# The expert inputs' transposes go from DMA to TensorE for pairs 18 to 111

## The reference

```python
xn = _layernorm(x)                                   # [8, 512, 256]
# s: attention over columns: softmax(q^T k / sqrt(8)), 256 x 256 per batch
q, k, v = xn @ Wq, xn @ Wk, xn @ Wv
s = swap(softmax(swap(q) @ k / sqrt(8)) @ swap(v)) @ Wo
# f: 32 experts, each row goes to 6 of them (chosen within its 3 best groups of 4)
scores = softmax(xn @ gate_weight.T)
combine = top 6 of the scores in the top 3 of 8 groups, divided by their sum
y = sum over e of combine[:, e] * ((silu(xn @ w1[e].T) * (xn @ w3[e].T)) @ w2[e].T)
shared = silu(xn @ sw1.T) * (xn @ sw3.T) @ sw2.T
out = x + s * silu(y + shared)
```

## Time and profile before

| | us |
|---|---|
| median of 3 runs | 707.58 (707.14 to 709.71) |
| the profiled execution | 710.04 |
| its span, first to last instruction | 708.3 |
| PE busy | 536.7 (76%) |
| DVE busy | 436.6 (62%) |
| POOL busy | 379.8 (54%) |
| ACT busy | 303.8 (43%) |

### The profile page before, as it was taken

One profiled execution on the slowest core, in us unless ns is written; L12 is line 12 of the kernel. 1 busy time (PEld: TensorE's weight loads), 2 busy tenths in 40 slices (PEclk: granted clock), 3 DMA queues, 4 the chain that ended last, 5 costly groups with the idle time before them and its releaser, 6 DMA issues.

```text
span 708.3 us, 12537 instructions
## 1 busy us (share of the span) xinstructions
PE 536.7 (76%) x3308; PEld 386.9 (55%) x3308; DVE 436.6 (62%) x1380; ACT 303.8 (43%) x626; POOL 379.8 (54%) x401
## 2 busy tenths in 40 slices
PE   7687885959586787842999888887887877888860
PEld 6465664647374666521877565554554545655540
DVE  7976786959595958860332355565564556555566
ACT  5434654554545453521454334334333344343341
POOL 1175665666656666763002655565555656655654
PEclk9868998989899798955999989999999999999995
DMA  9999392938484343533999999999999999999975
GB/s 328 413 393 397 154 390 94 355 149 303 188 287 173 119 171 112 174 123 104 219 236 217 224 284 271 256 297 288 269 268 274 289 247 266 303 288 274 268 231 168
DMA packets 216514, 174.69 MB, mean 247 GB/s; under 512 B 128770, under 2 KB 201218, under 8 KB 215554
## 3 DMA queue, kind: packets, MB, share of 16 engines
q1 hardware_dynamic: 192514, 108.30, 59.7%
q0 software_dynamic: 18432, 50.36, 21.4%
q10 hardware_dynamic: 5504, 15.24, 5.8%
HBM read 52.20 MB, written 92.27 MB: 204 GB/s over the span
## 4 chain that ended last, share of the span: by engine, by line
PE 41%; another core or an unknown queue 18%; ACT 15%; issue 12%; DVE 10%; DMA 2%; POOL 2%; ACTq 0%; POOLq 0%; DVEq 0%; SPq 0%
PE ps L760 11%; PE ps L780 8%; PE ps L675 7%; PE ps L659 6%; PE ps L667 3%; ACT early L616 3%; PE ps L681 3%; PE ps L770 2%; ACT work L594 2%; ACT work L609 2%; DVE work L1062 1%; POOL early L454 1%; DVE acc L1043 1%; ACT L535 1%
## 5 line engine op out<-in xcount | busy, mean ns | idle before, releaser
L454 POOL DMA_INDIRECT early<-slots_d,slot_at x192 | 186.6, 972 | 184.3 <-DMA slots_d<-early 58.0
L760 PE MATMUL ps<-w_all,work 128*128 x1344 | 190.0, 281 | 41.3 <-issue 27.1
L760 PEld LDWEIGHTS ps<-w_all,work 128*128 128x128 f16 x1344 | 115.6, 100 | 106.3 <-issue 80.8
L1062 DVE SCALAR_TENSOR_TENSOR work<-ps,work 128x256 f32<-128x256 f32 x112 | 47.2, 421 | 180.3 <-ACT work L594 172.2
L436 POOL DMA_INDIRECT slots_d<-early,slot_at x96 | 96.0, 1000 | 80.2 <-DVE slot_at L914 29.4
L436 POOL DMA_INDIRECT slots_d<-work,slot_at x96 | 95.0, 990 | 55.2 <-issue 25.4
L594 ACT ACTIVATE work<-ps 128x256 f32<-128x256 f32 x112 | 43.7, 390 | 170.2 <-remote 110.6
L780 PE MATMUL ps<-w_all,work 128*128 x672 | 96.2, 281 | 5.9 <-DVE work L1067 4.7
L616 ACT ACTIVATE early<-ps 128x512 f32<-128x512 f32 x112 | 67.1, 600 | 41.4 <-PE ps L780 30.3
L1043 DVE SCALAR_TENSOR_TENSOR acc<-early,wk,acc 128x256 f32<-128x256 f32 x160 | 77.8, 486 | 4.2 <-DMA early<-slots_d,slot_at 0.4
L659 PE MATMUL ps<-early,work 128*128 128x256 f32 x128 | 42.3, 488 | 47.4 <-ACT work L479 47.4
(11 more groups left out here) (148 smaller groups left out, 678.1 us busy)
## 6 DMA issues: line engine op xcount, KB each, us to landing
slots_d<-early SPq DMA_DIRECT2D x112, 256.0 KB
slots_d<-pad SPq DMA_DIRECT2D x7, 3072.0 KB
w_all<-in_wexp ACTq DMA_DIRECT2D x7, 1536.0 KB
slots_d<-work SPq DMA_DIRECT2D x1, 5120.0 KB, 19.2
s_all<-in_x SPq DMA_DIRECT2D x8, 512.0 KB, 6.3
ysh_d<-work ACTq DMA_DIRECT2D x8, 512.0 KB
early<-ysh_d SPq DMA_DIRECT2D x32, 128.0 KB
early<-in_x SPq DMA_DIRECT2D x32, 128.0 KB
```

What stands on the lines that cost most here:

```text
L454: pool.indirect_dma_start(gath[:, at % GATH_RING, :], None, slots_d[:, :], bass.IndirectOffsetOnAxis(ap=slot_at[:, rank_of(at):rank_of(at) ...
L760: mm = pe.matmul(ps[:, 2 + p % 2, h * 2 * I:(h + 1) * 2 * I], xT[:, p % DEEP, x_low * HC + k, h * P:(h + 1) * P], w16[:, bass.ds(at + (w_l ...
```

## The change

Pairs 0 to 17 (`BY_DMA = 18`) are loaded as before. For pairs from 18 on:

- SP loads the pair's rows with a plain DMA into `slot`, the same six places untransposed. From pair 24 on the load waits for `s_eT_ps` (the place's rows are turned) instead of `s_eab_ps`.
- TensorE gets a new stage `turn_rows`, three pairs ahead, between `expert_out` and `hidden`: eight fp16 transposes of 128 x 128 with an fp16 identity into PSUM bank p%2 (0 or 1), the last incrementing `s_eT_ps`.
- ScalarE (`copy_even`) or VectorE (`copy_odd`) copies the bank, 128 x 1024 fp16, to one of two places `xT_on`, as the first thing of its step (on VectorE behind `sums`), two pairs ahead. It waits for the first layer of pair p-2, which read that place.
- `hidden` waits for that copy (`s_eT`) instead of the DMA.
- VectorE makes `ident16` once, early in stage 1.

```diff
+BY_DMA = 18
@@ load_slots
-                if p >= DEEP:
+                if p >= BY_DMA + DEEP:
+                    sp.wait_ge(s_eT_ps, p - DEEP - BY_DMA + 1)
+                elif p >= DEEP:
                     sp.wait_ge(s_eab_ps, p - DEEP + 1)
-                sp.dma_start_transpose(xT[:, k], slots16_d[p * (2 * P):(p + 1) * (2 * P), :]).then_inc(s_slot[k], 16)
+                if p < BY_DMA:
+                    sp.dma_start_transpose(xT[:, k], slots16_d[p * (2 * P):(p + 1) * (2 * P), :]).then_inc(s_slot[k], 16)
+                else:
+                    sp.dma_start(slot[:, 2 * k:2 * k + 2, :], rows_of_pair(p)).then_inc(s_slot[k], 16)
@@ ScalarE
+            def copy_even(p):
+                if p >= BY_DMA and p % 2 == 0:
+                    act.wait_ge(s_eab_ps, p - 1)
+                    act.wait_ge(s_eT_ps, p - BY_DMA + 1)
+                    act.activation(xT_on[0].rearrange("p c n -> p (c n)"), turned_pair(p), ACT.Copy).then_inc(s_eT[0], 1)
-            in_steps((silu, 1, PAIRS), (gate, -BEHIND, GATHER_PAIRS), (turned_hidden, 0, PAIRS),
+            in_steps((copy_even, 2, PAIRS), (silu, 1, PAIRS), (gate, -BEHIND, GATHER_PAIRS), (turned_hidden, 0, PAIRS),
@@ TensorE
+            def turn_rows(p):
+                if p >= BY_DMA:
+                    if p >= BY_DMA + 2:
+                        pe.wait_ge(s_eT[p % 2], copies(p - 2))
+                    pe.wait_ge(s_slot[p % DEEP], p // DEEP * 16 + 16)
+                    for low in range(2):
+                        for c in range(HC):
+                            for h in range(2):
+                                at = ((low * HC + c) * 2 + h) * P
+                                mm = pe.transpose(turned_pair(p)[:, at:at + P],
+                                                  slot16[:, 2 * (p % DEEP) + h, low, c * P:(c + 1) * P], ident16[:])
+                    mm.then_inc(s_eT_ps, 1)
             def hidden(p):
-                pe.wait_ge(s_slot[p % DEEP], p // DEEP * 16 + 16)
+                if p < BY_DMA:
+                    pe.wait_ge(s_slot[p % DEEP], p // DEEP * 16 + 16)
+                else:
+                    pe.wait_ge(s_eT[p % 2], copies(p))
+                x_halves = xT[:, p % DEEP] if p < BY_DMA else xT_on[p % 2]
-            in_steps((turn_hidden, 0, PAIRS), (expert_out, -1, PAIRS), (hidden, 2, PAIRS))
+            in_steps((turn_hidden, 0, PAIRS), (expert_out, -1, PAIRS), (turn_rows, 3, PAIRS), (hidden, 2, PAIRS))
@@ VectorE
+            dve.tensor_copy(ident16[:], ident[:]).then_inc(s_ident16, 1)
+            def copy_odd(p):
+                if p >= BY_DMA and p % 2 == 1:
+                    dve.wait_ge(s_eab_ps, p - 1)
+                    dve.wait_ge(s_eT_ps, p - BY_DMA + 1)
+                    dve.tensor_copy(xT_on[1].rearrange("p c n -> p (c n)"), turned_pair(p)).then_inc(s_eT[1], 1)
-            in_steps((sums, -BEHIND, GATHER_PAIRS), (hidden_rows, 1, PAIRS), (low_hidden, 0, PAIRS))
+            in_steps((sums, -BEHIND, GATHER_PAIRS), (copy_odd, 2, PAIRS), (hidden_rows, 1, PAIRS), (low_hidden, 0, PAIRS))
```

More of the change, by code:

```diff
@@ L134, in gated_attention_moe @@
         ident = sb("ident", [P, P])
+        ident16 = sb("ident16", [P, P], F16)
         tri = sb("tri", [P, P], BF16)
@@ L149, in gated_attention_moe @@
         mx, nmx, rsum, rinv = (sb(n, [P, HC]) for n in ("mx", "nmx", "rsum", "rinv"))
+        slot = part(0, RING * H, RING)
         xT = part(0, RING * H).bitcast(F16).rearrange("p (k c n) -> p k c n", k=DEEP, c=2 * HC)
+        slot16 = part(0, RING * H).bitcast(F16).rearrange("p (k s c) -> p k s c", k=RING, s=2)
         at = RING * H
+        xT_on = [part(at + 2 * H * k, 2 * H).bitcast(F16).rearrange("p (c n) -> p c n", c=2 * HC) for k in range(2)]
+        at += 4 * H
         silu_e, h_e = ([part(at + (2 * n + k) * 2 * I, 2 * I, 2) for k in range(2)] for n in range(2))
@@ L209, in gated_attention_moe @@
         s_const = sem("s_const")
+        s_ident16 = sem("s_ident16")
         s_w = sem("s_w")
@@ L262, in gated_attention_moe @@
         s_slot = sems("s_slot", DEEP)
-        s_eab_ps, s_ehT_ps, s_ey_ps = (sem(n) for n in ("s_eab_ps", "s_ehT_ps", "s_ey_ps"))
-        s_esilu, s_eh = (sem(n) for n in ("s_esilu", "s_eh"))
+        s_eT_ps, s_eab_ps, s_ehT_ps, s_ey_ps = (sem(n) for n in ("s_eT_ps", "s_eab_ps", "s_ehT_ps", "s_ey_ps"))
+        s_eT, s_esilu, s_eh = sems("s_eT", 2), sem("s_esilu"), sem("s_eh")
         s_ehThi, s_ehT, s_ey = (sem(n) for n in ("s_ehThi", "s_ehT", "s_ey"))
@@ L285, in raw_weights, with turned_pair, copies @@
             return w_all[:, (b + 1) * (EB * WEXP):(b + 2) * (EB * WEXP)].rearrange("p (e c) -> p e c", e=EB)
+        def turned_pair(p):
+            return ps[:, p % 2, :].bitcast(F16)
+        def copies(p):
+            return (p - BY_DMA) // 2 + 1
         def rank_of(at):
@@ L735, in _ @@
                 batch(b)
+            pe.wait_ge(s_ident16, 1)
             pe.wait_ge(s_tables, 16)
@@ L759, in hidden @@
                         for n, (x_low, w_low) in enumerate(SHARED):
-                            mm = pe.matmul(ps[:, 2 + p % 2, h * 2 * I:(h + 1) * 2 * I], xT[:, p % DEEP, x_low * HC + k, h * P:(h + 1) * P],
+                            mm = pe.matmul(ps[:, 2 + p % 2, h * 2 * I:(h + 1) * 2 * I], x_halves[:, x_low * HC + k, h * P:(h + 1) * P],
                                            w16[:, bass.ds(at + (w_low * WEXP + k * 2 * I), 2 * I)],
```

## The result

The changed kernel takes 713.54 us (median of 20 runs, 710.21 to 717.37) where the kernel before takes 706.7 beside it (20 runs, 701.52 to 713.3): a ratio of 1.0104, 95% interval 1.0084 to 1.0125. So it is slower, by 6.8 us and not by the 16.4 of the forecast. The profiled execution took 713.62 us, 1.7 around its span of 711.9.

The account below looks back on a forecast made before the run. Bound: TensorE's increments kept during GpSimd's back-to-back indirect DMAs. Mixed long and short cycles give 3.51 us a pair against 3.345: +15.0 us for 91 pairs, +1.5 for pairs 18 to 20, so 724 us; range 668 to 738.

Parts of the forecast that it names:

- The direction and the bound: Whole kernel: slower, 724 us, as TensorE's increments are kept while GpSimd writes indirect DMAs back to back; slower given 0.51.
- the fixed number of instructions in a run: Gather stage: TensorE gets some 103 instructions in a run of four gathers, then stops; two pairs now need 143.4.
- a long cycle: Gather stage: four gathers, pause and restart take 6.64 us and carry 1.67 pairs, while the gathers ask for 2.
- The short cycle: Gather stage: two gathers and one pair, 2.22+1.24+0.67 = 4.13 us, with TensorE time for 1.53 pairs.
- the rival of no change: Gather stage: GpSimd's cycle still has four gathers and two pairs, TensorE's idle time takes the transposes; 709 us, chance 0.14.
- the prediction's sentence on the held copy: Copy for pair s+2: if TensorE's increment is held, copy and the first layer behind it start only at the release; unsized.
- The rival of a faster kernel: Gather stage: the keeping of increments shortens with the DMA load; 679 us if half the 1.24 us goes; chance 0.34.
- the end of that rival: Gather stage: the keeping of increments vanishes altogether and TensorE's 2.7 us a pair bounds; 650 us, chance about 0.1.
- Transposes: TensorE from pair 18 on: eight fp16 transposes at 0.06 us each, 0.5 us a pair (0.44 to 0.88).
- ScalarE's copy: ScalarE on even pairs: copying 1024 elements takes 1.04 us, 0.52 a pair.
- VectorE's copy: VectorE on odd pairs: copying 1024 elements takes at most 1.28 us, at the lower end half of it.
- The load's wait for `s_eT_ps`: SP's loads from pair 24 on: waiting one step sooner leaves five steps of 3.3 us cover; worth nothing by itself.

Follow-up runs that it names:

- e8: The changed kernel with the 192 gathers as plain DMAs issued by GpSimd, rows not the chosen ones: 640.88 us, ratio 0.9087 to the kernel before.
- e11: Kernel before with plain loads for all pairs, unread transposes from pair 18, no copies, on a chip of the first kind: 702.06 us, ratio 0.9926.
- e3: Kernel before with plain loads for all pairs and eight unread transposes a pair, no copies, on a chip of the second kind: 612.25 us, ratio 0.9308.
- e10: The changed kernel with one small memset on GpSimd behind every gather: 715.36 us, ratio 1.0135 to the kernel before.
- e12: The changed kernel unchanged, run again on a chip of the first kind: 712.51 us, ratio 1.0079 to the kernel before.
- e9: The changed kernel with a pair's transposes one pair earlier in TensorE's order: 710.88 us, ratio 1.0058 to the kernel before.
- e16: The changed kernel unchanged, run again on a chip of the second kind: 611.69 us, ratio 0.9358 to the kernel before.
- e6: The changed kernel unchanged, run again on another chip of the first kind: 712.19 us, ratio 1.0109 to the kernel before.

## Why the prediction was right and wrong

**The direction and the bound: right, the direction partly by luck.** Increments of TensorE kept back beside runs of indirect DMAs set the pace of both kernels on that chip; e8, with plain gathers, shows them gone, and e11 beside e3 that the same kernel takes 702 us where they are kept and 612 where they aren't. But the loss was forecast from two terms, and neither had its size.

**The step that failed: the fixed number of instructions in a run**, which made a long cycle carry 1.67 pairs. By it TensorE should have stopped at about the same count (some 37 matmuls), "now inside the transposes". It did 12+2+6+8+12+2+5 = 47 matmuls from 501.26 on and then stopped, in the second layer, at 505.48 + 0.71 = 506.19. The reading that the count came from was incomplete as well. Between the nine matmuls that end at 511.74 and the one at 512.67 stand two more, which the earlier trace rows leaves out:

```profile
511.93 0.38 PE L760 MATMUL ps<-w_all,work 128*128 x2 [0.19 <-issue]
```

So the stop at 37 was one of 0.19 us, and a longer one, of 0.36 us, came at 39.

One cycle of each kernel proves little, so I take all runs of four from 388 to 684 us (gathers less than 0.5 us apart counted as one run), and in each TensorE's first stop of 0.15 us or more for "issue" from 3.5 us on. The kernel before has one in 26 of 35 runs, at a median of 34 matmuls (middle half 34 to 37) and 99 instructions; the kernel after in 26 of 27, at 50 matmuls (49 to 52) and 138 instructions. The count is not fixed. The time moved less, from 4.9 us into the run (4.6 to 5.1) to 5.4 (5.3 to 5.5). What does stay is **the time of the release**, measured from the run's start and not from its end: 512.71 - 506.74 = 5.97 us before, 507.11 - 501.13 = 5.98 after, 5.96 in e10. Over the runs of four, the first wait for "remote" that ends over 5.5 us into the run ends at a median of 5.97 us before, 5.94 after, 5.93 in e11 and 5.95 in e10, while the median run of gathers lasts 4.74, 4.94, 4.75 and 5.10 us. So the release follows neither TensorE's count nor the length of the row of gathers, and within 6.4 us of a run's start TensorE has done its 56 matmuls, two pairs, in most long cycles of the kernel after. What grew is the time from the release to GpSimd's next gather, from 0.68 us to 0.80, and with it the long cycle, from 6.68 us on average to 6.74.

**The short cycle was mis-sized too.** The forecast gave it 4.13 us. GpSimd early in the gather stage of the kernel after:

```profile
389.18 0.95 POOL L473 DMA_INDIRECT early<-slots_d,slot_at  x1 [0.98 <-remote]
390.43 0.95 POOL L473 DMA_INDIRECT early<-slots_d,slot_at  x1 [0.31 <-issue]
392.36 0.95 POOL L473 DMA_INDIRECT early<-slots_d,slot_at  x1 [0.98 <-remote]
```

392.36 - 389.18 = 3.18 us for two gathers and one pair, no worse than half a long cycle. I had carried over the 1.24 and 0.67 us behind a run of four; behind a run of two it is 0.98 us in all. Later runs of two take longer, so that all 24 of them from 388 to 684 us average 3.43 us, beside 28 runs of four at 6.74. A pair then takes 3.43 or 6.74/2 = 3.37 us, whichever cycle it is in, and the measured 3.402 lies between, where the forecast had 3.51. That runs of two would stand beside runs of four was forecast rightly: before, there were 4 of two and 35 of four.

**The nearest case was the rival of no change**, given 0.14: a cycle with four gathers still carries two pairs, because TensorE's idle 0.6 us a pair takes the transposes. It gave 709; 5.2 us more come from the 0.057 us a pair. e12 against e11 puts a price on what that rival left out: the copies, 10.45 us, partly paid by the 5.4 us that plain loads and transposes gain there. That they cost by their place behind a kept increment, as the prediction's sentence on the held copy had it without a number in the sum, fits TensorE's 24.9 + 7.4 us of waits for them and their smaller cost on the other kind of chip (about 3 us); e9, which moved the trip, gained nothing clear, and no run on this kind of chip changed their length.

**The rival of a faster kernel was right about another chip and wrong about this one.** It had the kept increments shorten with the DMA load. The share fell from 1.12 to 0.86 and the release still came 5.9 us behind the run's start; e11, at 0.90, says the same. On the chips that keep nothing back the transposing loads set the pace, and there the gain comes to 42 us (e16): TensorE's own work as the bound (2.79 us a pair measured, 2.7 forecast), the end of that rival that I gave about 0.1.

**The terms.** *Transposes:* one takes 0.22 us and eight in a row 0.61, so they start some 0.055 us apart, 0.44 us a pair; 0.06 had been taken. The 81 ns of the Trainium skill ("TensorE: Matmul & The Clock Gate", "Back-to-back issue gap"), which would have added 2 us, doesn't fit them. *ScalarE's copy:* 1.04 us, as forecast. *VectorE's copy:* 0.689 us, near the lower end of 0.64 to 1.28. It is fp16 out of PSUM, 1.9 times as fast by the element as the fp32 rows of 512 at 0.64, which are another operation. The Trainium skill ("VectorE: DVE Perf Modes", "Why PSUM operands drop a tier") says that an operand in PSUM allows at most the doubled rate and fp32 none; the trace is in line with both. *The load's wait for `s_eT_ps`:* no wait of TensorE's for `work<-slots_d` shows in the list after; right.

**What stays open.** What keeps the increments, why they come out 5.9 to 6.0 us behind the start of a run of four, and why chips 10 and 12 and the one of the result do this and 6, 9 and 13 don't. The transposes alone were not measured on the first kind of chip, so the 5.4 us of e11 can't be split. No run lengthened a gather or left a long pause between two, so whether GpSimd's stopping plays a part in the release isn't shown.

## What to carry to other kernels

When a table of waits names no releaser, look for an engine whose unbroken rows of work go with it, and read the stop both as a count and as a time, over many cycles, before building a sum on one of them. Work that is added to an engine which stands idle inside someone else's cycle can cost little: e11 carries the transposes and is still 5.4 us under the kernel before. A new trip from that engine to another and back did cost, 10.45 us on the chip with kept increments. And a change that shifts load from one resource to another can have opposite signs on two chips: time it on more than one before a verdict.

## What the runs showed of the hardware

Two kinds of chip, by these kernels: the kernel before at 705 to 707 us on two chips and 654 to 658 on three. On the second kind GpSimd's indirect DMAs take the same 0.94 us, and TensorE's increments arrive at once, beside a row of 79 of them in e16. The dispatch stage differs too: the first gather starts at 381.3 us in e6 and at 347.8 in e16, the same kernel. The granted clock is not the cause in the gather stage (0.99 in e6's window, 0.98 in e16's). From 0 to 330 us it is 0.85 in e6 and 0.90 in e16, so there it may have a share in the difference, beside e6's waits for "remote".

On the first kind, beside a run of four indirect gathers, waits put down to "remote" end 5.9 to 6.1 us behind the run's start (medians of the eight kernels traced with such gathers), and register operations of TensorE that otherwise take 46 ns take up to 0.92 us.

Plain DMAs that GpSimd issues (0.54 us each, 0.97 for indirect ones) went with no kept increment on a chip that keeps them beside indirect ones. And of a memset of 0.22 us on GpSimd between two indirect DMAs, about two thirds fitted into the 0.30 us that lie between them anyway.
